# An attention and mixture-of-experts kernel: experts' rows padded to 64 instead of 128, in 64 full slots and 8 mixed ones

## The chip, the cores and the metric

The kernel runs on one core of a Trainium2 chip. The engines are TensorE (PE, with its weight loads shown apart as PEld), VectorE (DVE), ScalarE (ACT), GpSimd (POOL) and SyncE (SP); SP and ACT issue direct transfers on a queue of their own, POOL issues the indexed ones. The metric is the device time of one execution in microseconds (us), median of the runs. In the profile a float32 matmul stands as two records (each goes over its columns twice), so four matmuls are eight records.

## What is computed

A layer on T = 2048 tokens of width 512: layer norm, a gated-delta attention with 8 heads and its residual, a second layer norm, and then a mixture of 16 experts, 4 of them per token, beside a shared expert. The part that matters:

```python
cw = _combine_weights(xt, gate_w)            # [T, 16], four nonzero per token
out = jnp.zeros_like(xt)
for e in range(16):
    a = _swiglu(xt @ expert_up_w[e].T)       # 512 -> 2 x 352 -> 352
    out = out + cw[:, e:e + 1] * (a @ expert_down_w[e].T)   # 352 -> 512
out = out + _swiglu(xt @ shared_up_w.T) @ shared_down_w.T
x = x + out
```

All of it is float32. With the inputs of the reference the 16 experts get 521, 591, 568, 472, 458, 474, 495, 434, 522, 578, 522, 527, 510, 482, 495 and 543 rows, 8192 together; these counts are worked out from the reference and stand in no profile.

## The kernel before

**The order of the work.** The attention runs first (`attention`), with pieces of the shared expert between its matmuls. `experts` then finishes the shared expert (`up`, `down`, `gated`), routes the rows (`routing`: VectorE makes for every row and choice its position in `slot_rows`, and the lists that say which expert a slot has), and GpSimd scatters the rows to `slot_rows` with 64 indexed transfers (L2064). Then come the slots.

**A slot** is 128 rows of one expert. `NQ` = 79 slots are always run: 64 full tiles' worth of rows and 15 for padding, since every expert is padded to a multiple of 128. With the counts above 72 of them hold rows and the last seven are empty; they cost TensorE the same. Every engine walks through `body(q, par)` for all q, by `run_slots` (straight code for the first two and last slots, a loop over pairs between). For one slot:

- TensorE: `gate` (4 matmuls of 352 columns, L2289), `up` (4 of 352, L2298), and then `down` of the slot before (3 of 512, L2314). Gate q waits for `xsT` (s_xT), up q for `a` of the slot before (s_a), down q-1 for its 16 transposed blocks (s_aT).
- ScalarE, in this order: issue the four transfers that load the rows of slot q+2 (`load_rows`, L2106, `xs`, packets of 512 B), issue the small one with weights and indices of slot q+1 (`load_meta`, L2113), SiLU of gate q (L2129), and y of slot q-1 (L2140), scaled out of PSUM.
- VectorE: transpose the rows of slot q+1 (L2175, `xsT`), a = g * up (L2208), transpose a in 16 blocks (L2187), take the combine weights and indices (L2198, L2199).
- GpSimd: one indexed transfer adds the 128 rows of y to `out` (L2079, "rows_added" s_add); each waits for the one before, since two may touch the same row. Rows whose index is out of bounds are left out.
- SyncE: holds three experts' weights in `w` (NS = 3) and loads expert s into w[s % 3] with three transfers (`load_expert`, L32 to L36), once the last slot of expert s-3 is through TensorE (s_yp against the list `tiles_to`). One expert is 512 x 704 and 352 x 512 float32, 2.16 MB.

The list of experts by slot is made by VectorE in `routing` behind the positions (L1896 to L1907).

Of the kernel before, what the change touches and what calls it, by code (L numbers as in the profile page):

```python
# [1781 lines left out]
NQ = K * T // P + E - 1  # L1782
assert NQ % 2 == 1
NS = 3

def routing(nc, es, counts, scratch, lg, xall, pos, qslot, qexp, tiles_to, s_pos, s_read, s_routed, route, s_xall):
# [21 lines left out]
    nti, idle = sb("nti", [P, E], I32), sb("silu_first", [P, E])  # L1808
    nt, one_e, tinc, posf = part(E), part(E), part(E), part(NT, E)
    pj, ids = part(NT, K), part(NT)  # L1810
    idi = sb("idi", [P, NT], I32)
    qi, qc = sb("qi", [1, NQ]), both[0:1, 0:NQ * E].rearrange("p (q e) -> p q e", e=E)
    qf, q3 = sb("qf", [1, NQ]), sb("q3", [1, NQ])
# [10 lines left out]
    def route_pool(pool):  # L1824
        pool.memset(before[:, :], 1.0).then_inc(s_k, 1)
        pool.memset(ones[:, :], 1.0).then_inc(s_k, 1)
        pool.iota(qi[:, :], pattern=[[1, NQ]], base=0, channel_multiplier=0,
# [15 lines left out]

    def route_dve(dve):
        n = [0]

        def mark(ins):
            ins.then_inc(s_d, 1)
            n[0] += 1
# [9 lines left out]
        for step in range(7):  # L1859
# [12 lines left out]
        link(dve.tensor_tensor(cnt[:, :, :], inc[:, :, :], cnt[:, :, :], ALU.subtract))  # L1872

        link(dve.tensor_scalar(nti[:, :], inc[:, :, NT - 1], float(P - 1), None, ALU.add))
        link(dve.tensor_scalar(nti[:, :], nti[:, :], 7, None, ALU.logical_shift_right))
        link(dve.tensor_scalar(nt[:, :], nti[:, :], 1.0, None, ALU.max))
        link(dve.tensor_tensor_scan(tinc[:, :], one_e[:, :], nt[:, :], 0.0, ALU.mult, ALU.add))
        link(dve.tensor_copy(tiles_to[:, :], tinc[0:1, :]))
        link(dve.tensor_tensor(nt[:, :], tinc[:, :], nt[:, :], ALU.subtract))
        link(dve.scalar_tensor_tensor(out=cnt[:, :, :], in0=nt[:, :].unsqueeze(2).to_broadcast([P, E, NT]),  # L1880
                                      scalar=float(P), in1=cnt[:, :, :], op0=ALU.mult, op1=ALU.add))
        dve.tensor_tensor(posf[:, :, :], pre[:, :].rearrange("p (t e) -> p t e", e=E),
                          cnt[:, :, :].rearrange("p e t -> p t e"), ALU.add).then_inc(s_read, 1)
        dve.wait_ge(s_read, 1)
        for j in range(K):
# [10 lines left out]
        dve.wait_ge(s_k, 4)  # L1896
        link(dve.tensor_tensor(qc[:, :, :], qi[:, :].unsqueeze(2).to_broadcast([1, NQ, E]),
                               tinc[0:1, :].unsqueeze(1).to_broadcast([1, NQ, E]), ALU.is_ge))
        link(dve.tensor_reduce(qf[:, :], qc[:, :, :], AX.X, ALU.add))  # L1899
        link(dve.tensor_scalar(qf[:, :], qf[:, :], float(E - 1), None, ALU.min))  # L1900
        link(dve.tensor_copy(qexp[:, :], qf[:, :]))

        link(dve.tensor_copy(q3[:, :], qf[:, :]))
        for m in range(NS, E, NS):
            link(dve.tensor_scalar(qc[:, :, 0], qf[:, :], float(m), -float(NS), ALU.is_ge, ALU.mult))
            link(dve.tensor_tensor(q3[:, :], q3[:, :], qc[:, :, 0], ALU.add))
        dve.tensor_copy(qslot[:, :], q3[:, :]).then_inc(s_routed, 1)  # L1907

    return route_act, route_pool, route_pe, route_dve


def experts(nc, es, wup_d, wdn_d, xs_d, acc_d, x2n_d, xT_d, lg, pos, qslot, qexp, tiles_to, wsh, route, sh, out):
# [11 lines left out]
    w = sb("w", [P, NS, UPW + DNW])  # L1924
    acc = sb("acc_all", [P, NT - EARLY_TILES, D])
# [48 lines left out]
    def first(q):  # L1974
        return isinstance(q, int) and q == 0
# [433 lines left out]
```

## Time and profile before

| | us |
|---|---|
| median of 3 runs (1309.14 to 1313.19) | 1310.31 |
| span of the profiled execution | 1306.4 |
| TensorE busy, share of the span | 1264.5, 97% |
| VectorE, ScalarE, GpSimd busy | 872.4, 375.1, 340.0 |
| from the first slot's gate to the end | 588.0 (718.4 to 1306.4) |

The profiled execution's span is 3.9 us under the median. The profile shows one execution; "busy" of TensorE is modelled from pipelined records. "Granted clock" 1.00 is 2.4 GHz, 0.50 is 1.2 GHz.

### The profile page before, as it was taken

Reading aid. Unit: us, or ns where it says so; the run is one execution under the profiler, and the core shown is the slowest. Engines: PE = TensorE matmul, PEld = TensorE weight load, DVE = VectorE, ACT = ScalarE, POOL = GpSimd, SP = SyncE. Lnnn points to the kernel's source line nnn. Section 1 sums busy time; section 2 is a strip of 40 time slices with the busy share of each in tenths; the row PEclk is TensorE's granted clock in tenths of the full one; section 3 lists DMA queues with packets and bytes.
Section 4 is the critical chain, followed back from the end, with each engine's and each line's share of the span. In section 5 each row is a group of like instructions: output and inputs, shape, how many; then the busy total and the mean of one; then the engine's idle time right before and its main releaser. Section 6 shows DMA issues by size and latency. Waiting matters only on the chain.

```text
span 1306.4 us, 27873 instructions
## 1 busy us (share of the span) xinstructions
PE 1264.5 (97%) x8725; PEld 787.1 (60%) x8726; DVE 872.4 (67%) x2430; ACT 375.1 (29%) x822; POOL 340.0 (26%) x398
## 2 busy tenths in 40 slices
PE   8969999999999999999999999999999999999997
PEld 7857778777775555444444555555555555555553
DVE  4897688768768465262111777777777777777774
ACT  4745655645553333210000111111111111111111
POOL 1301234313242231225651112121212122121212
PEclk9989999999997999999999999999999999999999
DMA  5524944743643694585467456666665656564420
GB/s 163 95 47 99 157 94 101 166 105 85 138 109 114 169 199 116 124 274 199 182 211 246 85 130 138 134 137 137 137 139 133 135 132 136 127 139 72 75 49 9
DMA packets 208516, 171.09 MB, mean 131 GB/s; under 512 B 71472, under 2 KB 160560, under 8 KB 208432
## 3 DMA queue, kind: packets, MB, share of 16 engines
q1 hardware_dynamic: 135056, 114.16, 33.9%
q0 software_dynamic: 16496, 34.23, 13.4%
q10 hardware_dynamic: 56880, 21.54, 7.9%
q8 instruction: 57, 0.93, 0.3%
q14 instruction: 27, 0.22, 0.1%
HBM read 91.06 MB, written 82.73 MB: 133 GB/s over the span
## 4 chain that ended last, share of the span: by engine, by line
PE 55%; DVE 2%; issue 0%; DMA 0%; POOL 0%; ACT 0%; DVEq 0%; POOLq 0%
PE pD L2314 15%; PE pG L2289 14%; PE pU L2298 14%; PE pG L2246 3%; PE pU L2246 3%; PE pD L2265 3%; PE pU L2240 1%; PE pD L2260 0%; DVE ups L2187 0%; DMA out<-y,ix 0%; DVE w L1887 0%; DVE w L1888 0%; DVE route_keep L1886 0%; POOL out L2079 0%; DVE qf L1899 0%
## 5 line engine op out<-in xcount | busy, mean ns | idle before, releaser
L2187 DVE STREAM_TRANSPOSE ups<-a 32x96 f32<-32x96 f32 (+1 forms) x1248 | 326.1, 261 | 42.5
L2079 POOL DMA_INDIRECT out<-y,ix x79 | 123.0, 1557 | 479.1 <-ACT y L2140 319.4
L2314 PE MATMUL pD<-w,ups 128*128 (+1 forms) x474 | 216.6, 592 | 0.7 <-DVE ups L2187 0.7
L2289 PE MATMUL pG<-w,xsT 128*128 x632 | 199.9, 458 | 0.0
L2298 PE MATMUL pU<-w,xsT 128*128 x632 | 199.9, 459 | 0.0
L2289 PEld LDWEIGHTS pG<-w,xsT 128*128 128x128 f32 x632 | 119.5, 189 | 88.4 <-issue 37.4
L2298 PEld LDWEIGHTS pU<-w,xsT 128*128 128x128 f32 x632 | 120.1, 190 | 66.9
L976 PE MATMUL pProj<-front_region 128*128 128x256 f32 x624 | 154.8, 391 | 2.2 <-ACT front_region L711 1.6
L2314 PEld LDWEIGHTS pD<-w,ups 128*128 128x128 f32 (+1 forms) x474 | 90.0, 190 | 93.2 <-issue 76.8
L976 PEld LDWEIGHTS pProj<-front_region 128*128 128x128 f32 x624 | 113.3, 191 | 20.1 <-ACT front_region L711 2.1
L2140 ACT ACTIVATE y<-pD,wq 128x512 f32<-128x512 f32 x79 | 54.3, 687 | 247.0 <-PE pD L2314 234.1
L2129 ACT ACTIVATE g<-pG 128x352 f32<-128x352 f32 x79 | 36.7, 464 | 259.9 <-DVE ix L2199 132.0
L1399 DVE SCALAR_TENSOR_TENSOR front_region<-front_region,cw 128x256 f32<-128x256 f32 x216 | 102.6, 516 | 8.8 <-ACT front_region L747 6.3
L2208 DVE TENSOR_TENSOR a<-g,pU 128x352 f32<-128x352 f32 x79 | 41.2, 521 | 87.2 <-PE pU L2298 79.4
L2064 POOL DMA_INDIRECT slot_rows<-xall,pos x64 | 62.9, 982 | 52.3 <-DMA slot_rows<-xall,pos 47.1
L636 POOL TENSOR_TENSOR TT<-TT,ng 128x512 f32<-128x512 f32 x16 | 17.3, 1082 | 213.7 <-ACT TT L789 137.3
L2175 DVE STREAM_TRANSPOSE xsT<-xs 128x512 f32<-128x512 f32 x79 | 55.9, 708 | 6.2 <-DMA xs<-slot_rows 5.0
L1175 PE MATMUL pT<-wo,oT 128*128 128x512 f32 x128 | 59.1, 604 | 0.4 <-ACT oT L816 0.4
L2265 PE MATMUL pD<-front_region 128*128 128x512 f32 x120 | 53.1, 597 | 0.0
L746 ACT ACTIVATE front_region<-pProj 128x256 f32<-128x256 f32 x78 | 30.1, 386 | 79.0 <-PE pProj L976 76.8
L1461 DVE TENSOR_TENSOR Rs<-pC,vh 64x512 f32<-64x512 f32 x32 | 22.0, 687 | 45.3 <-PE pC L1086 45.0
L2246 PE MATMUL pG<-front_region 128*128 128x512 f32 x112 | 50.4, 593 | 0.6 <-PEq L383 0.6
(258 smaller groups left out, 1661.8 us busy)
## 6 DMA issues: line engine op xcount, KB each, us to landing
w<-in_up_T SPq DMA_DIRECT2D x16, 1408.0 KB
slot_rows<-zeros SPq DMA_DIRECT2D x79, 266.0 KB
xs<-slot_rows ACTq DMA_DIRECT2D x316, 64.0 KB
w<-in_down_T SPq DMA_DIRECT2D x16, 512.0 KB
front_region<-in_L_attn_hidden_states SPq DMA_DIRECT2D x16, 256.0 KB, 3.6
x2r<-in_L_attn_hidden_states SPq DMA_DIRECT2D x16, 256.0 KB, 4.5
partial_sums<-x2r SPq DMA_DIRECT2D x16, 256.0 KB, 2.9
x_normed<-x2n SPq DMA_DIRECT2D x16, 256.0 KB, 2.0
```

Of the source, the lines that this page charges most:

```text
L976: mm = pe.matmul(proj_bank(g), w3[:, w, k, cols(i % DC, P)], xnT[p % 2][:, k, :], start=(k == 0), stop=(k == DC - 1))
L1175: mm = pe.matmul(pT1[:, 0, :], oT[:, k, :], wo[:, k, :], start=(k == 0), stop=(k == DC - 1))
L1399: ins = dve.scalar_tensor_tensor(out=acc[(g + h) % len(acc)], in0=raw[:, at, j:j + PW], scalar=cw[:, at, j:j + 1], in1=acc[(g + h) % len(a ...
L2064: pool.indirect_dma_start(out=xs_d[:, :], out_offset=bass.IndirectOffsetOnAxis(ap=pos[:, i, j:j + 1], axis=0), in_=xall[:, i, :], in_offse ...
L2079: pool.indirect_dma_start(out=flat, out_offset=bass.IndirectOffsetOnAxis(ap=ix[1 - par][:, 0:1], axis=0), in_=y[1 - par][:, :], in_offset= ...
L2175: dve.transpose(xsT[par][:, :, :].rearrange("p k (a i) -> p a k i", a=BLOCKS), xs[par][:, :].rearrange("p (a k j) -> p a k j", a=BLOCKS, k ...
L2187: dve.transpose(aT[par][B * to:B * to + B, 0:n, rows], a[rows, 0:len(IC) * P].rearrange("p (c n) -> p c n", c=len(IC))[:, 0:n, B * to:B * ...
L2246: mm = pe.matmul(p[:, :], wsh["up"][:, k, at:at + P], xg[gr % 2][:, k, :], start=(k == 0), stop=(k == DC - 1))
L2265: mm = pe.matmul(sdown(j)[:, :], sa[:, c, P * i:P * i + P], wsh["down"][:, c, :], start=False, stop=(c == UNITS - 1))
L2289: mm = pe.matmul(pG[0][:, 0:I], xsT[par][:, k, :], w[:, bass.ds(slot, 1), 2 * I * k:2 * I * k + I], start=(k == 0), stop=(k == DC - 1))
L2298: mm = pe.matmul(pU[0][:, 0:I], xsT[par][:, k, :], w[:, bass.ds(slot, 1), 2 * I * k + I:2 * I * (k + 1)], start=(k == 0), stop=(k == DC - 1))
L2314: mm = pe.matmul((pYlast if end(q) else pYq)[:, :], aT[1 - par][0:m, c, :], down[0:m, :, UPW + D * c:UPW + D * (c + 1)], start=(c == 0), s ...
```

## The change

Rows of an expert are now padded to 64. An expert's whole 128-row blocks go to the 64 full slots (NF); what is left, at most 64 rows, goes to a half block, and 16 half blocks make 8 mixed slots (NM), each with two halves of any two experts. If the experts have more than 64 whole blocks together, the ones beyond go to half blocks as well. 72 slots are run instead of 79; every ninth slot, from q = 7, is mixed (7, 16, ..., 70), slot 71 is a full one.

- TensorE, mixed slot (`project`, `bring_down`): each matmul is made as two of 64 stationary columns, for rows 0 to 63 with the one expert's weights, and for rows 64 to 127 with the other's, written to the two halves of the PSUM partitions.
- Weights of mixed slots have a place of their own, `wm`, in the region that held the shared expert's weights. ScalarE issues their loads (`load_mixed`, two experts, six transfers) at the end of its body of slots 0, 9, 18, ..., 63, after y. The full slots' loads stay with SyncE, but their expert is now read from a list (`source`), and so is the slot after which they may start (`until`).
- GpSimd adds a mixed slot with two indexed transfers, one for each half, one after the other.
- `routing` has about 9 more small operations and 6 on 256 columns ahead of the positions; the lists are made in five pieces (`list_dve`) between VectorE's operations of the shared expert. s_routed now comes from the fifth, and all three first weight loads wait for it.
- The slots are written out straight instead of in a loop, and TensorE reads two register values for the slot before where it read one.

The core of the diff:

```diff
+HR = P // 2
+NF = K * T // P
+NM = E // 2
+NQ = NF + NM
+STEP = NQ // NM
+MIXED = STEP - 2
+def is_mixed(q):
+    return q % STEP == MIXED
+    wm = region[:, 0:2 * (UPW + DNW)].rearrange("p (h n) -> p h n", h=2)
@@ run_slots
-        with eng.Fori(1, (NQ - 3) // 2) as pair:
-            body(2 * pair, 0)
-            body(2 * pair + 1, 1)
+        for q in range(NQ + 1):
+            body(q, q % 2)
@@ sync
-                load_expert(sp, w[:, s % NS], wup_d[s], wdn_d[s], s_w)
+                load_expert(sp, w[:, s % NS], *weights_from(sp, "source", s), s_w)
@@ gpsimd
+                for h in range(2 if is_mixed(q - 1) else 1):
+                    to = ixm[h] if is_mixed(q - 1) else ix[1 - par]
+                    least(pool, s_add, 16 * (adds_before(q - 1) + h))
+                    pool.indirect_dma_start(...)
@@ scalar
+            def load_mixed(m):
+                for h in range(2):
+                    load_expert(act, wm[:, h], *weights_from(act, "mixed", 2 * m + h), s_wm)
@@ scalar, end of body(q, par)
+                if q % STEP == 0 and q < NQ:
+                    if first(q):
+                        act.wait_ge(s_routed, 1)
+                    load_mixed(q // STEP)
@@ tensor
+            def project(out, rows, q, weights, at):
+                if is_mixed(q):
+                    for k in range(DC):
+                        for h in range(2):
+                            half = slice(HR * h, HR * h + HR)
+                            mm = pe.matmul(out[half, 0:I], rows[:, k, half], wm[:, h, 2 * I * k + at:2 * I * k + at + I],
+                                           start=(k == 0), stop=(k == DC - 1))
+                    return mm
+            def bring_down(out, gated_, q, weights, c):
+                m, at = IC[c], UPW + D * c
+                if is_mixed(q):
+                    for h in range(2):
+                        half = slice(HR * h, HR * h + HR)
+                        mm = pe.matmul(out[half, :], gated_[0:m, c, half], wm[0:m, h, at:at + D],
+                                       start=(c == 0), stop=(c == 2))
+                    return mm
```

ScalarE's instructions from one y to the next, in the loop of before (`xs` the rows, `mt` weights and indices, `g` the SiLU; ISA rows are register work):

```order
L2140 ACTIVATE y<-pD,wq 128x512 [waits rows_added]
L2106 ISA [waits slotsT_ready]
L2106 DMA xs<-slot_rows 32x4x128
...
L2113 ISA [waits meta_taken]
L2113 DMA mt<-slot_rows 128x20
L2129 ACTIVATE g<-pG 128x352 [waits gated_ready,gate_psum]
```

And the same stretch of the changed kernel after slot 8's y, in the body of slot 9 (`front_region` holds `wm`):

```order
L2248 ACTIVATE y<-pD,wq 128x512 [waits rows_added,meta_taken,y_psum2]
L2092 TENSOR_LOAD list_mixed
L32 DMA front_region<-in_up_T 128x4x704
L34 DMA front_region<-in_down_T 128x2x512
L36 DMA front_region<-in_down_T 96x512
...
L2211 DMA xs<-slot_rows 32x4x128 [waits slotsT_ready]
L2211 DMA xs<-slot_rows 32x4x128 x3
L2217 DMA mt<-slot_rows 128x20 [waits meta_taken]
L2238 ACTIVATE g<-pG 128x352 [waits gated_ready,gate_psum]
```

Between y of slot 8 and the loads of slot 12's rows now stand the six transfers of two experts' weights, on the same queue.

TensorE's instructions at a mixed slot of the changed kernel, from its gate to the gate of the next (`pG`, `pU`, `pD` are the PSUM banks of gate, up and down):

```order
L2405 MATMUL pG<-front_region,xsT 64x352 [waits gate_silu,mixed_weights_loaded,slotsT_ready]
L2405 MATMUL pG<-front_region,xsT 64x352 x7
...
L2405 MATMUL pU<-front_region,xsT 64x352 [waits gated_ready]
L2405 MATMUL pU<-front_region,xsT 64x352 x7
L2422 ISA [waits y_ready,gatedT_ready]
L2422 MATMUL pD<-w,ups 128x512
...
L2409 MATMUL pG<-w,xsT 128x352
```

Eight half matmuls stand for four whole ones in gate and up, then the down of the full slot before; the mixed slot's own down (six half matmuls) follows after the next up.

## Rows read from the trace of the kernel before

**Rows 1.** The costliest groups: count, busy us, mean ns, and idle before.

```profile
L2314 PE MATMUL pD<-w,ups 128*128 (+1 forms) x474 | 216.6, 592 | 0.7 <-DVE ups L2187 0.7
```

**Rows 2.** Timeline of one slot: start, us, engine, line, what; idle before in brackets.

```profile
782.66 2.53 PE L2289 MATMUL pG<-w,xsT 128*128 x8
782.95 0.69 ACT L2140 ACTIVATE y<-pD,wq 128x512 f32<-128x512 f32 x1 [3.26 <-PE pD L2314]
...
788.31 4.64 DVE L2187 STREAM_TRANSPOSE ups<-a 32x96 f32<-32x96 f32 x16
...
789.98 2.53 PE L2289 MATMUL pG<-w,xsT 128*128 x8
...
793.15 0.71 DVE L2175 STREAM_TRANSPOSE xsT<-xs 128x512 f32<-128x512 f32 x1
...
794.71 2.74 PE L2314 MATMUL pD<-w,ups 128*128 x6
...
797.29 2.53 PE L2289 MATMUL pG<-w,xsT 128*128 x8
...
797.53 0.37 SPq L32 DMA_DIRECT2D w<-in_up_T  x1
```

**Rows 3.** Timeline, TensorE, four 64 x 64 tiles in turn.

```profile
35.68 0.69 PE L1037 MATMUL pG<-kq 64*64 64x64 f32 x32
36.30 0.48 PE L976 MATMUL pProj<-front_region 128*128 128x256 f32 x1
```

**Rows 4.** Timeline, TensorE: two row halves of 512 columns, then whole matmuls.

```profile
582.34 1.13 PE L2260 MATMUL pD<-front_region 64*128 64x512 f32 x4
583.40 1.12 PE L2265 MATMUL pD<-front_region 128*128 128x512 f32 x2
```

**Rows 5.** One line's weight loads, 64 columns: duration ns min/median/max.

```profile
L1189 PEld LDWEIGHTS pT<-gw,x2g x256: 132/138/227, 194.8 to 553.0; 128*64 128x64 f32 x128
```

**Rows 6.** Transfers issued from 555.9 to 562.9 us, median us from issue to landing.

```profile
front_region<-x2n_turned SPq DMA_DIRECT2D x4, 256.0 KB, 9.4
```

**Rows 7.** Transfers issued from 584 to 592 us.

```profile
front_region<-x2n_turned SPq DMA_DIRECT2D x4, 256.0 KB, 3.8
```

**Rows 8.** GB/s in 40 slices of 550 to 570 us.

```profile
GB/s 0 0 0 0 0 0 0 0 0 33 119 127 111 397 397 389 414 373 377 303 393 418 397 324 389 414 393 389 354 339 323 299 292 291 295 320 359 393 381 389
```

**Rows 9.** Transfers during an expert's weight load, 797 to 805 us, 40 slices.

```profile
GB/s 0 0 0 0 0 0 0 84 113 84 70 99 282 324 296 261 284 370 413 399 397 419 342 385 352 411 410 404 348 310 344 312 298 327 335 353 315 318 279 333
...
out<-y,ix POOLq DMA_INDIRECT x1, 8.1
```

**Rows 10.** The page: adds, median us to landing.

```profile
out<-y,ix POOLq DMA_INDIRECT x79, 4.8
```

**Rows 11.** Adds issued from 1285 to 1306 us.

```profile
out<-y,ix POOLq DMA_INDIRECT x3, 2.7
```

**Rows 12.** Timeline, the last two adds.

```profile
1296.56 1.56 POOL L2079 DMA_INDIRECT out<-y,ix  x1 [6.09 <-ACT y L2140]
...
1300.19 1.55 POOL L2079 DMA_INDIRECT out<-y,ix  x1 [2.07 <-DMA out<-y,ix]
```

**Rows 13.** TensorE by stretches: length, busy (records), granted clock, transfers' share, GB/s.

```profile
87.50:90.50 3.00, 0.03 (x1) 0.99 0.00 0
90.50:93.20 2.70, 0.02 (x1) 0.50 0.00 0
93.20:97.30 4.10, 4.10 (x41) 0.50 0.01 4
...
298.70:302.10 3.40, 3.40 (x26) 0.50 0.67 141
```

**Rows 14.** Register reads of the slot list: duration ns min/median/max.

```profile
L2270 PEldq TENSOR_LOAD <-qslot x79: 296/305/987, 706.9 to 1283.2; - x79
```

**Rows 15.** Timeline, VectorE: a routing operation on 256 columns, slot 0's rows.

```profile
577.30 0.42 DVE L1872 TENSOR_TENSOR w<-w 128x256 f32<-128x256 f32 x1
...
711.27 0.71 DVE L2175 STREAM_TRANSPOSE xsT<-xs 128x512 f32<-128x512 f32 x1 [1.77 <-DMA xs<-slot_rows]
```

More of the change, by code:

```diff
@@ L1781, with before_mixed, adds_before, block_of @@
 NE = E + 2
-NQ = K * T // P + E - 1
-assert NQ % 2 == 1
-NS = 3
-def routing(nc, es, counts, scratch, lg, xall, pos, qslot, qexp, tiles_to, s_pos, s_read, s_routed, route, s_xall):
+HR = P // 2
[4 more added lines that the diff above has]
+MIXED = STEP - 2
+NS = 3
+def is_mixed(q):
+    return q % STEP == MIXED
+def before_mixed(q):
+    return max(0, (q + STEP - 1 - MIXED) // STEP)
+def adds_before(q):
+    return q + before_mixed(q)
+def block_of(q):
+    return NF + q // STEP if is_mixed(q) else q - before_mixed(q)
+assert sorted(block_of(q) for q in range(NQ)) == list(range(NQ))
+assert all(q == i + (i + 1) // 8 for q in range(NQ) if not is_mixed(q) for i in [block_of(q)])
+def routing(nc, es, counts, scratch, lg, xall, pos, lists, s_pos, s_read, s_routed, route, s_xall):
     def sb(name, shape, dt=F32):
@@ L1807, in routing @@
     cnt, seg, inc = part(E, NT), part(E, NT), part(E, NT)
-    nti, idle = sb("nti", [P, E], I32), sb("silu_first", [P, E])
-    nt, one_e, tinc, posf = part(E), part(E), part(E), part(NT, E)
+    hti, fti, idle = sb("hti", [P, E], I32), sb("fti", [P, E], I32), sb("silu_first", [P, E])
+    hf, ff, of, cumf, cumo, one_e = (part(E) for _ in range(6))
+    full_rows, odd_at, apart, over, posf = part(E), part(E), part(E), part(1), part(NT, E)
     pj, ids = part(NT, K), part(NT)
     idi = sb("idi", [P, NT], I32)
-    qi, qc = sb("qi", [1, NQ]), both[0:1, 0:NQ * E].rearrange("p (q e) -> p q e", e=E)
-    qf, q3 = sb("qf", [1, NQ]), sb("q3", [1, NQ])
+    qi, qc = sb("qi", [1, NF]), both[0:1, 0:NF * E].rearrange("p (q e) -> p q e", e=E)
+    qf, qa, q3 = sb("qf", [1, NF]), sb("qa", [1, NF]), sb("q3", [1, NF])
+    cap, had, some, nth, twice, le, lm, lo_ = (sb(n, [1, E]) for n in (
+        "cap", "had", "some", "nth", "twice", "list_e", "list_m", "list_o"))
+    done_i = sb("done_i", [1, E], I32)
     pre, tot = counts[:, 0:NT * E], counts[:, NT * E:2 * NT * E]
@@ L1914, in experts @@
+    return route_act, route_pool, route_pe, route_dve, list_dve
+def experts(nc, es, wup_d, wdn_d, xs_d, acc_d, x2n_d, xT_d, lg, pos, lists, region, wsh, route, sh, out):
     N = GN
@@ L2121, in body @@
                     load_rows(1, 1)
-                if not (isinstance(q, int) and q >= NQ - 2):
+                if q < NQ - 2:
                     load_rows(q + 2, par)
@@ L2334, in program @@
         pos = es.enter_context(nc.sbuf_tensor("pos", [P, NT, K], I32))
-        qslot = es.enter_context(nc.sbuf_tensor("qslot", [1, NQ], I32))
-        qexp = es.enter_context(nc.sbuf_tensor("qexp", [1, NQ], I32))
-        tiles_to = es.enter_context(nc.sbuf_tensor("tiles_to", [1, E], I32))
+        lists = {name: es.enter_context(nc.sbuf_tensor(f"list_{name}", [1, n], I32)) for name, n in (
+            ("slot", NF), ("load", NF), ("expert", NF), ("source", E), ("until", E), ("mixed", E))}
         xs_d = nc.dram_tensor("slot_rows", (NQ * P, RW), F32, kind="Internal").ap()
```

267 lines of the change are left out of this document (168 added, 99 removed).

## The prediction

> **What bounds the kernel now.** I read the costliest groups first, then the timeline of one slot. TensorE does: its largest group waited 0.7 us in 474 records [rows 1], and in the slots one gate begins 7.31 us after the other (782.66, 789.98, 797.29) with gate, up and down end to end [rows 2]. The other engines fit into that time. For what the change adds on the queues I need more: how long after ScalarE's y of a slot q-1 (T0, 782.95) the next steps are due [rows 2]. The gate beside it, at 782.66, is that of slot q+1, so the gate at 797.29 is that of slot q+3: due at T0+14.34. VectorE transposes its rows at T0+10.2. VectorE's 16 transposes take 4.64 and end at T0+10.0, the down that needs them starts at T0+11.76: 1.8 us of slack.
>
> **The change, part by part.**
>
> *Seven slots less.* 79 become 72, at 7.31 each: -51.2 us, all on TensorE's path.
>
> *Half matmuls.* A mixed slot has twice the matmuls, of 64 stationary columns each. It costs nothing more if the two halves run at the same time. Nothing before has column halves with long operands; the nearest are 16 matmuls on four tiles of 64 x 64 (two row halves times two column halves) [rows 3]: 32 records, each of 64 columns gone over twice (128 cycles at 2.4 GHz, 0.053), would be 1.7 us one after the other and 0.85 if only the row halves ran together; they take 0.62. So column halves do run together, and I take 7.31 for a mixed slot. To it comes the change of tiling: two row halves of 512 columns hold TensorE from 582.34 to 583.40, 1.06, where two rounds of 1024 cycles need 0.85 [rows 4]: 0.2 per change. A mixed slot changes four times (into gate and up, out, into its down, out): 0.8 x 8 = +6.4, bounds 0 and 6.4.
>
> *Adds.* A mixed slot has two, in turn. In the middle the second lands about 11 us after the slot's y (two steps of 3.6 to 4.8 and a landing [rows 10, 12]), and what waits for it lies within VectorE's 1.8 us of slack: 0, at most 1 us per slot. At the end it counts: slot 70 is mixed, and slot 71's add stands behind both. One add more is 3.63 us [rows 12]; and the last add had no rows before (2.7 us to landing [rows 11]) and has rows now (4.8 [rows 10]), 2.1. Sum +5.7.
>
> *Routing.* Six operations on 256 columns at about 0.45 [rows 15] and some nine small ones make the scatter 4 us later, and with it slot 0's rows. They were there at 711.27 [rows 15], the gate at 718.4: covered, 0; without that cover it would be +4. The lists lie between operations of an idle VectorE, and the register reads (0.3 us, at most 0.99 [rows 14]) are done by TensorE's sequencer while matmuls run: 0.
>
> *The mixed weights' loads.* This is the term that decides. ScalarE issues 2 x 2.16 = 4.33 MB right after y of slot q-1, q = 0, 9, ..., 63, and behind it, on the same queue, the rows of slot q+3. What does a small transfer behind large ones cost? Four of 256 KB took 9.4 us to landing behind 3 MB of SyncE's own, against 3.8 with nothing large ahead [rows 6, 7]. So a queue is served in order, and the rows wait for the last byte of both experts. The rate of large transfers alone is about 389 GB/s [rows 8].
> Without another load: first byte at T0+2.3 (a register read, the issue, and 1.0 us as SyncE's load shows, issued at 797.53 and seen from 798.5 [rows 2, 9]); 4.33 MB and one add's 0.26 MB take 11.8, T0+14.1; the rows' 512 small packets and their landing 1.4; the transpose 0.8 [rows 2]: T0+16.3 against 14.34, 2.0 late. VectorE then makes a (0.5) and its transposes (4.64), 0.5 more than gate and up cover: 2.5 us.
> With an expert's load of SyncE beside it: from the reference's counts the full blocks give loads after slots 4, 10, 14, 19, 23, 28, 32, 36, 40, 46, 50, 55 and 59 are done, the mixed ones start after 9, 18, 27, 36, 45, 54 and 63. So six of the seven (not 63) meet one: five times it comes 7.3 us later, once at the same time. First byte T0+9.3; by then 2.46 MB of the mixed weights are in, 1.87 remain, and shared in equal parts this takes 2 x 1.87 + 0.26 (an add) = 4.0 MB, 10.3 us, T0+19.6. Rows T0+21.0, transposed T0+21.8: 7.5 late, and 0.5 for the transposes, 8.0. The sixth comes to the same within 1 us.
> The load of slot 0 starts at 722 with gate 3 due at 738.8, late enough: 0. Sum 6 x 8.0 + 2.5 = +50.5. Bounds: 0, if the rows were not held up, and 6 x 10 + 5 = 65, if adds and issue stretch it.
>
> *The clock.* TensorE stands still some 7 us in each of the six. Before, a still stretch of 5.7 us ended with a granted clock of 0.50, and 4.1 us of work then ran at it; another fall lasted 3.4 us, busy throughout [rows 13]. Half speed for 4.1 us costs 2.05, of which 0.5 hides the wait for the transposes: 6 x 1.55 = +9.3, bounds 0 and 15.
>
> *Sum.* 1306.4 - 51.2 + 6.4 + 5.7 + 50.5 + 9.3 = 1327.1 of span; the median stood 3.9 over the span: 1331.
>
> **A rule weighed.** TensorE's weight loads of 64 columns took 0.138 [rows 5], and in rows 3 they hide behind the matmuls, since 4 tiles with loads and matmuls keep 0.62 for 32 records. The Trainium skill, "TensorE: Matmul & The Clock Gate", Part 3 on packing small matmuls, says that a weight load overlaps with matmuls in flight only where the row group differs; two column halves share all rows. The trace disagrees (0.62 us in rows 3). By the rule the sum would be rival C's first time, by the trace it stays.
>
> **Rivals.**
> *A, faster: the rows are not held up much.* Place: gate q+3 in the bodies of slots 9 to 63. If the six transfers leave gaps that the rows use, or SyncE's load gets less than an equal part, each of seven stalls is 2.5 at most and the clock stays up: 1306.4 - 51.2 + 6.4 + 5.7 + 17.5 + 3.9 = 1289, and 1271 with none. For it: under SyncE's load ScalarE's rows still came, since they are on another queue. Against: rows 6. It decides from an average of 6.5 us per met load, clock included: above, the kernel is slower than before.
> *B, the stalls are half as long (4.5 us),* since an add or the rows need less: 27 + 2.5, half the clock's price: 1306.4 - 51.2 + 6.4 + 5.7 + 29.5 + 5 + 3.9 = 1306.
> *C, it doesn't do what it says: column halves don't overlap in full.* Weight loads exposed: a mixed slot has 22 rounds, 22 x 0.138 x 8 = 24 more, 1355. Halves one after the other: 8 x 7.3 = 58 more, 1389. Against both: rows 3; for them: no operand there is longer than 64 columns.
>
> **How the numbers follow.** Forecast 0.54 (1316 to 1346), A 0.24 (1270 to 1297), B 0.13 (1298 to 1315), C 0.09 (1347 to 1395). A measurement of this kernel tells about 0.3% from no change: faster is under 1306.4, slower over 1314.2. Faster: A and 0.07 of B, 0.31; same 0.06; slower 0.63. The range leaves out the lower third of A and most of C: 1283 to 1358.
>
> **What would show it.** Right: after slots 9, 18, ..., 54 TensorE stands for 6 to 9 us at the gate three slots on, with VectorE's `xsT` waiting for the transfer of `xs`, and ScalarE's queue moving 4.3 MB just before; granted clock 0.50 there; about 2 us after slot 63, nothing after slot 0. A mixed slot's gate as long as a full one's (2.35 us from start to start). Last add about 5 us later behind the last y than before. Wrong: stalls under 4 us with the rows landing within 16 us of y (A, B); 64-column records that start alone, one after the other, or a mixed slot of more than 9 us (C); or slot 0's rows later than its gate.

## The result, and the profile of the changed kernel

| | before | changed |
|---|---|---|
| median of four runs, us | 1310.66 (1309.14 to 1313.19) | 1364.18 (1358.73 to 1366.32) |
| span of the profiled execution | 1306.4 | 1357.0 |

The ratio is 1.0405, 95% interval 1.0379 to 1.0431: slower by 4%. The prediction said 1331 and a range of 1283 to 1358. The direction was right, the size was not. The profiled execution of the changed kernel is the fastest of its four (1358.73), 5.5 us under their median, so the spans differ by 50.6 and the medians by 53.5. The page of the changed kernel (busy us and share; then the chain that ended last, by engine and by line):

```profile
span 1357.0 us, 25907 instructions
...
PE 1245.9 (92%) x8747; PEld 757.5 (56%) x8747; DVE 845.2 (62%) x2352; ACT 366.0 (27%) x808; POOL 340.4 (25%) x401
...
PE 43%; DMA 8%; ACTq 5%; issue 1%; DVE 0%; ACT 0%; POOLq 0%
PE pD L2422 9%; PE pG L2409 9%; PE pU L2409 8%; DMA xs<-slot_rows 8%; PE pD L2390 4%; PE pG L2371 4%; PE pU L2371 4%; ACTq L2211 2%; PE pD L2419 2%; PE pG L2405 1%; PE pU L2405 1%; ACTq L34 1%; ACTq L36 1%; ACTq L32 1%; PE pU L2365 1%
```

TensorE's busy time fell by 18.6 us, far less than the 51.2 of seven slots, because part of what is left ran at half speed (the same instructions are busy for 1221.1 us in the kernel of the first experiment, where TensorE hardly waits, and for 1245.9 here); and the chain now holds the rows' transfer and ScalarE's own issuing (ACTq). The waits of TensorE in the slots (engine, line, releaser: us in all, times, longest):

```profile
PE pG L2409 <- ACT g L2238: 45.8, 7, 11.3
PE pG L2409 <- DVE xsT L2287: 18.7, 7, 4.8
```

Seven mixed loads, each with a stall at gate q+2, and behind six of them a second one at gate q+3 (the seventh wait for `xsT`, 0.41 us at slot 3, is not behind one of these loads; the load after slot 62's y has only the first stall, 3.14). This is the first, after slot 8's y (timeline: start, us, engine, line; idle before in brackets), to be read beside [rows 2]:

```profile
794.55 2.53 PE L2409 MATMUL pG<-w,xsT 128*128 x8
794.75 0.69 ACT L2248 ACTIVATE y<-pD,wq 128x512 f32<-128x512 f32 x1 [3.79 <-PE pD L2422]
795.43 0.42 ACTq L32 DMA_DIRECT2D front_region<-in_up_T  x1
...
798.35 1.50 ACTq L34 DMA_DIRECT2D front_region<-in_down_T  x1
...
800.00 0.54 ACTq L36 DMA_DIRECT2D front_region<-in_down_T  x1
800.58 9.64 ACTq L2211 DMA_DIRECT2D xs<-slot_rows  x4
802.83 0.37 SPq L32 DMA_DIRECT2D w<-in_up_T  x1
...
810.26 1.46 ACTq L2217 DMA_DIRECT2D mt<-slot_rows  x1
811.83 0.46 ACT L2238 ACTIVATE g<-pG 128x352 f32<-128x352 f32 x1 [16.39 <-issue]
...
812.54 4.09 PE L2409 MATMUL pG<-w,xsT 128*128 x8 [10.52 <-ACT g L2238]
...
821.89 0.71 DVE L2287 STREAM_TRANSPOSE xsT<-xs 128x512 f32<-128x512 f32 x1 [4.12 <-DMA xs<-slot_rows]
...
823.05 2.63 PE L2409 MATMUL pG<-w,xsT 128*128 x8 [1.47 <-DVE xsT L2287]
```

The gate at 794.55 is slot q+1's (q = 9). Its SiLU, which stands in ScalarE's program behind all eleven issues, came at 811.83 and not at about 797. Of the 16.39 us before it, 9.64 went into issuing four transfers of 64 KB; without a large load ahead, the same four took 1.76. So **the engine that issues is held, not only the data**: gate q+2 waited 10.52 for g. Then the rows came late as well, and gate q+3 waited 1.47. This load is one of the two with the longest hold. From the first weight issue to the SiLU it is 9.0 to 16.9 us in the seven, and the hold does not always stand in the rows' issues, which took 2.8 to 5.6 behind the other six: at 1034.35 the six weight issues themselves took 10.2. The gate at 812.54 took 4.09 instead of 2.53: the clock had fallen.

```profile
core 0: us, PE busy (x), PEclk, DMA share, GB/s
801.50:811.70 10.20, 0.52 (x2) 0.69 1.04 351
812.60:815.00 2.40, 2.40 (x4) 0.50 1.05 324
```

Two terms of the prediction stand nearly as they were sized. A mixed slot, gate to gate 7.57 (772.01, 779.58) and 7.55 (779.58, 787.13), each some 0.25 over 7.31; the interval before these is 0.09 longer and the one behind them 0.11, 0.70 in all:

```profile
772.01 2.59 PE L2405 MATMUL pG<-front_region,xsT 128*64 128x352 f32 x16
774.43 2.54 PE L2405 MATMUL pU<-front_region,xsT 128*64 128x352 f32 x16
776.89 2.84 PE L2422 MATMUL pD<-w,ups 128*128 x6
779.58 2.53 PE L2409 MATMUL pG<-w,xsT 128*128 x8
...
784.40 2.80 PE L2419 MATMUL pD<-front_region,ups 128*64 128x512 f32 x12
787.13 2.63 PE L2409 MATMUL pG<-w,xsT 128*128 x8
```

Sixteen half records take 2.42 from start to start, where eight whole ones take 2.36: the halves overlap in full. And the end, three adds in turn, the last 5.74 us behind the start of the last y (before, the last add at 1300.19, [rows 12], stood 2.6 behind its y):

```profile
1341.47 1.56 POOL L2185 DMA_INDIRECT out<-y,ix_mixed  x1 [6.55 <-ACT y L2248]
1342.77 0.69 ACT L2248 ACTIVATE y<-pD,wq 128x512 f32<-128x512 f32 x1 [2.08 <-PE pD L2422]
1344.93 1.55 POOL L2185 DMA_INDIRECT out<-y,ix_mixed  x1 [1.91 <-DMA out<-y,ix_mixed]
1348.51 1.56 POOL L2185 DMA_INDIRECT out<-y,ix  x1 [2.02 <-DMA out<-y,ix_mixed]
```

### The profile page after: what moved, and what is told of

It reads as the page before. It is cut to its first block, busy times and chain, and to the rows that moved or that the text cites. A ratio compares the mean times of both kernels' runs of the same rounds, so it can differ in the third digit from the quotient of the medians.

```text
span 1357.0 us, 25907 instructions
## 1 busy us (share of the span) xinstructions
PE 1245.9 (92%) x8747; PEld 757.5 (56%) x8747; DVE 845.2 (62%) x2352; ACT 366.0 (27%) x808; POOL 340.4 (25%) x401
## 3 DMA queue, kind: packets, MB, share of 16 engines
q0 software_dynamic: 16640, 34.24, 12.2%
## 4 chain that ended last, share of the span: by engine, by line
PE 43%; DMA 8%; ACTq 5%; issue 1%; DVE 0%; ACT 0%; POOLq 0%
PE pD L2422 9%; PE pG L2409 9%; PE pU L2409 8%; DMA xs<-slot_rows 8%; PE pD L2390 4%; PE pG L2371 4%; PE pU L2371 4%; ACTq L2211 2%; PE pD L2419 2%; PE pG L2405 1%; PE pU L2405 1%; ACTq L34 1%; ACTq L36 1%; ACTq L32 1%; PE pU L2365 1%
## 5 line engine op out<-in xcount | busy, mean ns | idle before, releaser
L2298 DVE STREAM_TRANSPOSE ups<-a 32x96 f32<-32x96 f32 (+1 forms) x1136 | 296.9, 261 | 35.4
L2409 PE MATMUL pG<-w,xsT 128*128 x512 | 181.5, 501 | 64.6 <-ACT g L2238 45.8
L2185 POOL DMA_INDIRECT out<-y,ix x64 | 99.6, 1557 | 451.4 <-ACT y L2248 308.1
L2409 PEld LDWEIGHTS pG<-w,xsT 128*128 128x128 f32 x512 | 103.7, 206 | 149.9 <-issue 113.9
L2422 PE MATMUL pD<-w,ups 128*128 (+1 forms) x384 | 176.9, 596 | 0.7 <-DVE ups L2298 0.7
L2409 PE MATMUL pU<-w,xsT 128*128 x512 | 163.3, 462 | 0.0
L2409 PEld LDWEIGHTS pU<-w,xsT 128*128 128x128 f32 x512 | 98.6, 193 | 56.3 <-issue 3.8
L2422 PEld LDWEIGHTS pD<-w,ups 128*128 128x128 f32 (+1 forms) x384 | 71.8, 190 | 80.2 <-issue 70.2
L2248 ACT ACTIVATE y<-pD,wq 128x512 f32<-128x512 f32 x72 | 49.4, 687 | 198.3 <-PE pD L2422 174.4
L2287 DVE STREAM_TRANSPOSE xsT<-xs 128x512 f32<-128x512 f32 x72 | 50.8, 705 | 47.6 <-DMA xs<-slot_rows 47.4
```

Of the source, the lines that this page charges most:

```text
L2185: pool.indirect_dma_start(out=flat, out_offset=bass.IndirectOffsetOnAxis(ap=to[:, 0:1], axis=0), in_=y[1 - par][:, :], in_offset=None, bou ...
L2248: act.activation(y[1 - par][:, :], (pYlast if end(q) else pYq)[:, :], ACT.Copy, scale=wq[1 - par][:, 0:1]).then_inc(s_y, 1)
L2287: dve.transpose(xsT[par][:, :, :].rearrange("p k (a i) -> p a k i", a=BLOCKS), xs[par][:, :].rearrange("p (a k j) -> p a k j", a=BLOCKS, k ...
L2298: dve.transpose(aT[par][B * to:B * to + B, 0:n, rows], a[rows, 0:len(IC) * P].rearrange("p (c n) -> p c n", c=len(IC))[:, 0:n, B * to:B * ...
L2409: mm = pe.matmul(out[:, 0:I], rows[:, k, :], w[:, bass.ds(weights[0], 1), 2 * I * k + at:2 * I * k + at + I], start=(k == 0), stop=(k == D ...
L2422: return pe.matmul(out[:, :], gated_[0:m, c, :], w[0:m, bass.ds(weights[0], 1), at:at + D], start=(c == 0), stop=(c == 2))
```

## Experiments

Each stands beside runs of the kernel before on the same chip (medians 1310.65 to 1311.24); ratios are to those. The edits shift lines by a few, so gate is L2409 in one kernel and L2411 or L2414 in another; names tell. A cut diff shows the core of an edit; where the same change touches several lines, only one kind of them stands here. Two theories at the start: **Q**, ScalarE's queue (a long queue holds the engine that issues, and the rows lie behind 4.3 MB); **B**, the bytes themselves, which share 16 DMA engines whoever issues them.

**The loads alone.** Only the first pair is loaded.

```diff
-                if q % STEP == 0 and q < NQ:
-                    if first(q):
-                        act.wait_ge(s_routed, 1)
-                    load_mixed(q // STEP)
+                if first(q):
+                    act.wait_ge(s_routed, 1)
+                    load_mixed(0)
```

> The changed kernel, but only the first mixed slot's two experts are loaded; the seven later mixed slots use them again (their rows are computed with the wrong experts, all else is as before). Both theories expect the time without what the seven loads cost: 1310.3 - 51.2 for seven slots + 5.6 for the changes of tiling + 5.4 for the adds at the end, 1270, within 1266 to 1276, with TensorE never waiting between slot 1 and slot 70. If the column halves or the straight code cost more than the trace of the changed kernel seems to show, it stays above 1285.

Measured 1270.25 (1269.23 to 1272.37), ratio 0.9693 (0.9668 to 0.9717); TensorE has one gap over 0.5 us in all slots (0.73, at slot 0). Seven later loads cost the whole 94 us between this and 1364. The rest of the change is worth 40.

**Another placement of the same bytes.** One expert three slots after the other:

```diff
-                if q % STEP == 0 and q < NQ:
+                if q % STEP in (0, 3) and q < NQ:
-                    load_mixed(q // STEP)
+                    load_mixed(q // STEP, q % STEP // 3)
```

> The changed kernel, with the second expert of a mixed slot loaded by ScalarE three slots after the first: same bytes, same queue, never more than 2.16 MB ahead of the rows. Theory Q (ScalarE's queue: its packets fill it, the issue of the next rows then holds ScalarE's instruction stream, and the rows lie behind 4.3 MB): 864 + 512 + 128 packets no longer fill the queue, no SiLU is late, and the rows lie behind 5.6 us of weights, with another 5.6 where SyncE loads an expert as well: 0 to 10 us of stalls in all, 1270 to 1282. Theory B (bytes: 34 MB more share 16 engines, whatever the queue and the place): as the changed kernel, 1350 to 1370.

On SyncE's queue:

```diff
+            def load_mixed(m):
+                least(sp, s_g, 1)
+                least(sp, s_yp, STEP * m)
+                for h in range(2):
+                    load_expert(sp, wm[:, h], *weights_from(sp, "mixed", 2 * m + h), s_wm)
+            ahead_of = {3: (0,), 4: (1,), 6: (2,), 8: (3,), 10: (4,), 12: (5,), 14: (6,)}
             for s in range(NS, E):
+                for m in ahead_of.get(s, ()):
+                    load_mixed(m)
...
+            load_mixed(NM - 1)
```

> The changed kernel, with the mixed slots' weights issued by SyncE, at the same slots and in one go as before, between the experts' loads. Theory Q: ScalarE's queue holds only rows and indices again, which share the engines with one stream of weights instead of lying behind it: no issue above 2 us on ScalarE, waits of TensorE under 15 us in all, 1270 to 1290 (adds are slower for longer, that is the upper end). Theory B: 1350 to 1370.

And in six pieces of 0.72 MB, still by ScalarE (`load_piece` issues two of the four chunks of up, or down, of one expert):

```diff
-                if q % STEP == 0 and q < NQ:
+                if q % STEP < 6 and q < NQ:
-                    load_mixed(q // STEP)
+                    load_piece(q // STEP, q % STEP)
```

> The changed kernel, with the two experts of a mixed slot loaded by ScalarE in six pieces of 0.72 MB, one each at the end of six slots in a row. Theory Q: a row's transfer lies behind 1.9 us of weights at most, inside the slack of 4 us: no wait of TensorE, 1268 to 1276. Theory B: the same bytes cost the same, 1350 to 1370.

Measured 1298.78 (1296.55 to 1304.83), 1296.96 (1295.37 to 1304.18) and 1301.56 (1301.28 to 1303.29); ratios 0.9899 (0.9873 to 0.9925), 0.9898 (0.9867 to 0.9930), 0.9930 (0.9906 to 0.9955). Both theories missed, from two sides. B is refuted as the main cause: the same seven pairs, 30.3 MB, cost 27 to 31 us over 1270 instead of 94. Q is right for two thirds, and something remains, of nearly the same size in three placements. It isn't the same thing in all three. With the loads on SyncE's queue TensorE waits at gates, 15.4 us in the slots:

```profile
PE pG L2411 <- ACT g L2244: 6.9, 7, 2.3
PE pG L2411 <- DMA w<-in_up_T: 4.4, 2, 2.4
PE pG L2411 <- DMA w<-in_down_T: 4.1, 2, 2.2
```

The waits put down to the weights are the SiLU's as well: each of these four gates starts 0.25 us after the end of a late SiLU (g from 957.84 for 0.46, the gate at 958.55), and that SiLU stood behind VectorE's index taking. With one expert at a time on ScalarE's queue, 12.2 of 21.7 us follow a late transposition of rows (`xsT`), so the rows still came late behind the queue. With six pieces no gate of a full slot waits for g at all: 13.6 us are at the mixed slots' own gates, all seven, and 11.6 at six gates that wait for `xsT`.

**What the halves cost.** In the one-load kernel, gate and up with the halves one after the other, and then with whole matmuls.

```diff
-                    for k in range(DC):
-                        for h in range(2):
+                    for h in range(2):
+                        for k in range(DC):
```

> The one-load kernel (only the first mixed pair is loaded, later mixed slots reuse it, so their rows meet the wrong experts), with gate and up of a mixed slot written as four matmuls of the one half and then four of the other, instead of in turn. Down stays in turn. If two halves overlap only where their matmuls stand next to each other: a full gate is 2.35 and a full up 2.35 from start to start, so the two become 4.7 longer per mixed slot, 38 us in eight, 1270 + 38 = 1308. If the hardware could run them together in any order, or if weight loads alone set the price: 1270 as before, down to 1267 with fewer alternations.

Measured 1282.10 (1280.69 to 1283.85), ratio 0.9776 (0.9754 to 0.9798): 12 more, neither 0 nor 38. TensorE's timeline of that kernel shows why (gate at 771.56, the next operation's first matmul at 774.04, while matmuls of the gate still start at 774.92):

```profile
771.56 2.93 PE L2404 MATMUL pG<-front_region,xsT 128*64 128x352 f32 x13
774.04 0.51 PE L2404 MATMUL pU<-front_region,xsT 128*64 128x352 f32 x1
774.33 0.46 PE L2404 MATMUL pG<-front_region,xsT 128*64 128x352 f32 x1
...
774.92 0.46 PE L2404 MATMUL pG<-front_region,xsT 128*64 128x352 f32 x1
774.98 2.88 PE L2404 MATMUL pU<-front_region,xsT 128*64 128x352 f32 x13
```

TensorE starts the second half while the last records of the first half still run, and up while gate does. The order in the code costs 1.34 per mixed slot from gate to gate (8.91 against 7.57), 1.5 by the medians, not 4.7.

```diff
-                    for k in range(DC):
-                        for h in range(2): ...
+                    for k in range(DC):
+                        mm = pe.matmul(out[:, 0:I], rows[:, k, :], wm[:, 0, ...], ...)
```

> The one-load kernel with whole matmuls (128 stationary columns, the first half's weights) in the mixed slots: leaves out that the second half has its own expert. It takes the whole price of halves away and nothing else. From the slots of the one-load kernel (y to y 0.70 more around a mixed slot) both theories expect 8 x 0.70 = 5.6 less: 1264.6. If nothing moves, the 0.70 was the two adds' or the table's; if 10 or more come off, halves cost something beyond their slots, such as the clock.

Measured 1268.22 (1264.84 to 1270.66), ratio 0.9663 (0.9638 to 0.9687). The mixed slot is back at 7.31 from gate to gate (774.70 to 782.01 to 789.32 in its trace); the median moved by 2, its interval touches that of the one-load kernel, and this profile has three small stalls more (0.74, 1.30 and 0.81 us) and its first gate 4.1 us later (721.97 against 717.86). The 0.70 per slot is confirmed in the trace, not by the medians.

**The remainder on SyncE's queue: who waits for what.** In the SyncE kernel VectorE waits 57.0 us, 26 times, for an add of y to land before it may take indices. So, without the adds of slots 0 to 68, and with deeper buffers:

```diff
-                if first(q):
+                if q - 1 < 69:
                     return
```

(and `adds_before`, which the waits go by, counts from slot 69 on).

> SyncE issues the mixed loads, as in the run before of that name (1297), and the indexed adds of slots 0 to 68 are left out, so that out lacks their rows; the last adds stay. Adds theory (what is left of the loads' price is that the weights' bytes slow the adds, whose ends VectorE's index taking waits for): 1270 to 1275, and no wait for them. Bytes theory (the rows of xs come late because the engines' share is short): 1288 to 1297, with xsT still waiting for xs; the adds' own bytes, 0.26 MB each, give back 1 or 2 at most.

```diff
-    y = [sb(f"y{i}", [P, D]) for i in range(2)]
+    y = [sb(f"y{i}", [P, D]) for i in range(2)] + [region[:, FRONT_W - D:FRONT_W]]
-                    least(act, s_add, 16 * adds_before(q - 2))
+                    least(act, s_add, 16 * adds_before(q - 3))
-                least(dve, s_add, 16 * adds_before(q - 1))
+                least(dve, s_add, 16 * adds_before(q - 2))
```

> SyncE issues the mixed loads, and y, wq and ix are three deep, so that taking indices and y of a slot wait for the adds two and three slots back instead of one and two. Nothing is left out. Adds theory: most of the 27 us between 1297 and 1270 comes back: 1270 to 1280, since the queue of adds catches up between loads. Bytes theory: 1290 to 1297.

Without adds: 1268.03 (1266.95 to 1271.69), ratio 0.9679 (0.9654 to 0.9703), all of the remainder gone, and no gate waits. Three deep: 1293.25 (1290.90 to 1293.59), ratio 0.9863 (0.9844 to 0.9882): 4 back, not 20, and the interval of the ratio overlaps that of two deep. I took the depth to be still too small, and made it four; beside it the same for the two kernels with ScalarE's loads.

> SyncE issues the mixed loads and y, wq and ix are four deep. Nothing is left out. With three deep the worst stall came where a mixed slot's two adds in turn, each of about 8 us under the weights' bytes, ended 6.9 us after VectorE wanted the indices' place. One slot more of room is 7.3 us. Adds theory: that stall and nearly all others go, 1270 to 1276 (1268 to 1272 as without adds or loads, plus a few steps of 0.5). Bytes theory (xs or the weights themselves late): 1285 to 1293, as three deep.

Measured 1297.03 (1292.99 to 1307.69), ratio 0.9880 (0.9854 to 0.9905). Wrong again: no gain. The trace is of the slowest of the five executions (1307.69), so its sizes are on the long side. The timeline shows what the depth can't mend (a mixed slot's two adds, VectorE's index taking, SiLU, gate):

```profile
941.11 1.57 POOL L2196 DMA_INDIRECT out<-y,ix_mixed  x1 [8.42 <-DMA out<-y,ix]
...
949.85 1.55 POOL L2196 DMA_INDIRECT out<-y,ix_mixed  x1 [7.17 <-DMA out<-y,ix_mixed]
...
957.56 0.15 DVE L2323 COPY wq<-mt 128x1 f32 x1 [9.27 <-DMA out<-y,ix_mixed]
...
958.19 1.56 POOL L2196 DMA_INDIRECT out<-front_region,ix  x1 [6.79 <-DVE ix L2324]
...
958.25 0.46 ACT L2244 ACTIVATE g<-pG 128x352 f32<-128x352 f32 x1 [11.96 <-DVE ix L2324]
...
958.96 2.71 PE L2411 MATMUL pG<-w,xsT 128*128 x4 [6.09 <-ACT g L2244]
```

From one add's issue to the next it is 8.74 and 8.34 us here, while TensorE makes a slot in 7.31. Over this trace, 80 adds are issued between 738.50 and 1297.41, a mean step of 7.07; 27 of the 79 steps are over 8 us (mean 9.5, while weights come in) and 43 are between 5.3 and 6.3. The chain of adds is a **second bound**: each waits for the one before, and it hardly pauses. Only nine of the 79 steps ended with GpSimd released by y; they took 54.8 us together, 3.8 more than steps of 5.7 would have. The three-deep kernel, whose trace is of its fastest execution, has the same picture: 79 steps in 545.6 us, mean 6.91, ten of them released by y, 6.3 us over steps of 5.7. TensorE's 72 slots need 532 (72 x 7.31 + 8 x 0.70).

> ScalarE issues the mixed loads in six pieces of 0.72 MB, one after each of six slots, as in the run before of that name (1302), now with y, wq and ix four deep. Adds theory: as there, most of the 30 us over 1270 comes back, 1270 to 1280. If ScalarE's share of issuing (its rows 2.2 us behind a piece) is what is left there: 1290 to 1302, with VectorE's xsT waiting for xs.

Measured 1301.72 (1298.48 to 1309.39), ratio 0.9917 (0.9895 to 0.9939), as with two deep (1301.56). Depth doesn't help here either, but not for the reason above: it is the second half of the expectation that came true. The chain of adds has room here (29 of its 79 steps were released by y, 44.7 us over steps of 5.7), and TensorE's waits in the slots are for something else:

```profile
PE pG L2414 <- issue: 16.4, 7, 3.8
PE pG L2418 <- DVE xsT L2296: 10.2, 6, 3.0
```

L2414 is a mixed slot's gate, and "issue" says that the profile shows no releaser; the time fits the landing of its own weights. At slot 16 the last piece was issued at 837.00 and landings took up to 7.4 us there; the gate, due at 842.5, started at 844.49. So the last piece very likely came too late for the slot that needs it. Pieces that start a slot earlier were not tried.

**Number, bytes or meeting?** Four deep, with one add per mixed slot (its second half's rows left out):

```diff
-                for h in range(2 if is_mixed(q - 1) else 1):
+                for h in range(1):
```

(and `adds_before(q)` is q).

> As the four-deep run with SyncE's mixed loads at the old place, but a mixed slot is added with one indexed transfer instead of two; the rows of its second half are left out. All weights are still loaded, 8 of 80 adds are gone. Chain theory: 72 adds at a mean of 6.9 need 497 us, less than TensorE's 533: 1270 to 1278. If it is the adds' bytes or what they do to the weights: the bytes fall by 5% alone, 1290 or more.

Measured 1264.58 (1263.28 to 1265.82), ratio 0.9644 (0.9627 to 0.9661). All weights are loaded, 72 adds instead of 80, and every gap but slot 0's 0.72 is gone. GpSimd now waits for y more often, which means that the chain has room. The rows below are for the two of four y buffers that go by that name, and 30.3 of the 84.4 us is the wait before the first add; over both names and without that one, y released 16 of 71 steps, with 91 us of idle GpSimd, against 9 of 79 steps with 41 us four deep with 80 adds.

```profile
POOL out L2196 <- DMA out<-y,ix: 145.6, 24, 9.3
...
POOL out L2196 <- ACT y L2254: 84.4, 10, 30.3
```

Of the 32 us under the four-deep kernel, one step, 3.6, is that the last add stands behind one less.

The pair's loads three slots later, away from the two adds of the mixed slot, four deep and two deep:

```diff
-                least(sp, s_yp, STEP * m)
+                least(sp, s_yp, STEP * m + 3 if m else 0)
-            ahead_of = {3: (0,), 4: (1,), 6: (2,), 8: (3,), 10: (4,), 12: (5,), 14: (6,)}
+            ahead_of = {3: (0,), 5: (1,), 7: (2,), 9: (3,), 11: (4,), 13: (5,), 15: (6,)}
```

> SyncE issues the mixed loads, y, wq and ix four deep, and the pair for mixed slot 9m+7 starts after slot 9m+2 instead of 9m-1, so not while the two adds of mixed slot 9m-2 run. Nothing is left out. In the four-deep run before (1297) a step from one add to the next took 8.3 to 11 us under weights and 5.6 to 6 between, and the 80 steps filled the slots' time, so that depth bought nothing. Chain theory (the adds, each waiting for the one before, are now the bound): bytes and number of adds are the same, so the mean step hardly falls; but the queue of adds is emptied before each load: 1275 to 1290. Burst theory (only the meeting of load and double add hurts): 1270 to 1276.

> SyncE issues the mixed loads after slot 9m+2, all buffers as in the changed kernel (two deep). Chain theory: the queue of adds can run only one slot late before VectorE waits for it, so more is lost than four deep: 1282 to 1300. Burst theory: 1270 to 1280. It tells whether the place or the depth does the work.

Measured 1291.55 (1289.02 to 1292.08), ratio 0.9847 (0.9828 to 0.9865), and 1292.71 (1292.33 to 1294.20), ratio 0.9865 (0.9848 to 0.9881). Against the old place (1297.03 and 1296.96) that gives some 4 to 5 us, and the intervals of the ratios overlap at each depth: the meeting of load and double add is a small part at most, and depth is worth nothing that can be told. The burst theory is out. Nothing is left out in either, and they are faster than both kernels: 1.3 to 1.5% under before.

**Back to the changed kernel.** With four deep, and without adds (edits as above), ScalarE's burst in place:

> The changed kernel as it is (ScalarE issues the six transfers at once) with y, wq and ix four deep: takes the adds out of its stalls and leaves ScalarE's queue. Queue theory for the changed kernel: its stalls start from ScalarE held in issuing and from rows behind 4.3 MB, not from adds, so little comes back: 1345 to 1364. If the adds were also what held the changed kernel: 1335 or less, as of the 94 us for loads 27 remained with the queue free.

> The changed kernel with ScalarE's burst, and the adds of slots 0 to 68 left out. Queue theory for the changed kernel: both stalls stay, 64 us of still TensorE and 20 of slow clock; the adds' 0.5 MB within each burst are gone: 1345 to 1362. If adds were a large part there too, as with the loads on SyncE (28 us): 1335 or less.

Measured 1364.24 (1358.26 to 1365.08), ratio 1.0391 (1.0358 to 1.0423), and 1349.89 (1347.21 to 1351.06), ratio 1.0290 (1.0271 to 1.0309). Without the adds 14 of the 94 us come back and 80 stay; TensorE's gaps go from 65 to 54. The adds also lengthen the hold: without them it is 7.9 to 12.1 us from the first weight issue to the SiLU. Then the hold itself, by the number of pieces:

```diff
-                  up.rearrange("(c p) n -> p c n", p=P)
+                  up.rearrange("(p c) n -> p (c n)", p=P)
```

(and the same for down's first 256 rows).

> The changed kernel, but each partition reads one run of consecutive rows of in_up_T (11 KB) and of in_down_T (4 KB), so the same bytes in 128 + 128 + 96 pieces per expert instead of 512 + 256 + 96; the mixed rows then meet weights in the wrong order. Pieces theory (ScalarE is held since its queue takes only so many pieces at once): the hold of 9.6 us in issuing xs shrinks to 2 or less, the stall at gate q+2 (64.5 us in all for it and 18.7 for the second) goes, the rows still lie behind the bytes: the second stall grows to about 8, 1330 to 1350 in all. Bytes theory: the hold is as long as before, 1358 to 1370; if long pieces are cut into short ones on the way, the same.

Measured 1366.49 (1361.93 to 1368.54), ratio 1.0407 (1.0380 to 1.0435): not faster at all, where I had forecast 1330 to 1350. But the two stalls trade places, as the pieces theory says. TensorE's waits and ScalarE's timeline in this kernel:

```profile
PE pG L2414 <- DVE xsT L2292: 65.5, 8, 11.2
PE pG L2414 <- ACT g L2243: 9.3, 7, 2.6
```

```profile
801.43 2.20 ACTq L2211 DMA_DIRECT2D xs<-slot_rows  x4
803.67 1.56 ACTq L2217 DMA_DIRECT2D mt<-slot_rows  x1
805.34 0.46 ACT L2243 ACTIVATE g<-pG 128x352 f32<-128x352 f32 x1 [8.45 <-issue]
...
807.03 10.07 ACTq L2211 DMA_DIRECT2D xs<-slot_rows  x3
...
824.04 0.71 DVE L2292 STREAM_TRANSPOSE xsT<-xs 128x512 f32<-128x512 f32 x1 [12.41 <-DMA xs<-slot_rows]
...
825.11 3.30 PE L2414 MATMUL pG<-w,xsT 128*128 x5 [11.09 <-DVE xsT L2292]
```

The first four xs issues take 2.20 instead of 9.64, so SiLU comes at 805.34, and in all seven loads 6.3 to 8.5 us behind the first weight issue instead of 9.0 to 16.9; the hold comes one body later (10.07 for three here, the longest of the seven); and the rows of slot q+3 land no sooner, since the same bytes are ahead of them. With the same bytes ahead, the transposition of slot q+3's rows ended 28.6 us after y here and 27.9 in the changed kernel. So in these two kernels the number of pieces decides when ScalarE is held, and the bytes ahead in the queue when the rows come; the late rows alone cost what both stalls cost together (74.8 us of waits here, 64.5 there).

## Why the prediction was off

| term, us | forecast | in the trace |
|---|---|---|
| seven slots less | -51.2 | -51.2 (slots of 7.31 in both) |
| mixed slots | +6.4 | +5.6 (8 x 0.70) |
| adds at the end | +5.7 | +5.4 |
| routing, front | 0 | +3.1 (not the change's, see below) |
| stalls | +50.5 | +64.5 |
| clock | +9.3 | +23.2 (what remains of the sum; TensorE's busy time is 24.8 over that of the one-load kernel) |
| span against 1306.4 | +20.7 | +50.6 |

- **Slots, halves, end: right.** Whole matmuls bring back 7.31. Rival C is refuted; rivals A and B, with smaller stalls, are out as well, though A's sum without any stall, 1271, is what the one-load kernel runs in (1270.25). The rule of the Trainium skill weighed in the prediction ("TensorE: Matmul & The Clock Gate", Part 3) doesn't hold here: by it, and with rival C's first price, a mixed slot would have cost some 3 us more, and it cost 0.70. Nor does this case agree with the same Part's statement that matmuls start strictly in order: with the halves in sequence, a matmul of up (774.04) starts before the last ones of gate (774.33 to 774.92).
- **Routing: 0 forecast, and 0 is right.** The first gate came 3.1 us later (721.50 against 718.44), but the one-load kernel, with the same routing, has it at 717.86, and the whole-matmul kernel at 721.97. Executions differ by that much before the slots: line 1175, in the attention, first runs at 150.6 before, 155.2 in the changed kernel and 151.4 and 155.8 in these two. Slot 0's rows were transposed at 716.35, 5.1 us ahead of the gate, so the cover held.
- **Stalls: the step that failed is that a load causes a single stall, of 8.0, at gate q+3.** Mechanism, place and trigger of that stall were right (rows in order behind 4.3 MB, SyncE's load beside it at T0+8), but it was taken for the only effect. I priced ScalarE's issues as if they cost their usual time, and did not ask what stands behind them in its own program: the SiLU of slot q+1, on which gate q+2 waits. Gate q+2 waited up to 11.3 us for it. What was forecast as six stalls of 8.0 and one of 2.5 came as 45.8 at gate q+2 behind seven loads and 18.3 at gate q+3 behind six, 9.2 per load. The rows' own delay was too small in the sum as well: transposed 27.9 us after y (821.89 + 0.71 less 794.75), where it had 21.8. That the total, 64.5, is still within the term's upper bound of 65 is luck: most of it is a stall that the prediction did not have. The long-packet kernel shows the forecast mechanism almost alone: six gaps of 7.5 to 11.2, mean 9.9, for the 8.0, and 4.7 for the 2.5 of the last load.
- **Clock: 1.55 per stall was mis-sized.** It took one short interval from before [rows 13], and the term's upper bound was 15. Most loads have two still stretches, and the granted clock was at 0.50 nine times, for 3.4 to 13.7 us, 61 us of the slots in all; some of that lies within the stretches and costs nothing. The loss is 23 by the sum.
- **Adds in the middle, "0, at most 1 us per slot": wrong.** Without them the changed kernel is 14 us faster. I had a landing of 8.1 under a load [rows 9] and used 3.6 to 4.8 for the step.

After all this the answer to where the expected gain went is: 1270 was there for the taking. Of the 94 us that eat it, about 67 go when the loads leave ScalarE's queue (1364 to 1297), and 65 when they stay on it with one expert at a time (1299), so it is the burst there that costs them. The 27 that are left on SyncE's queue go with the adds: a chain that the extra weights slow and the eight extra adds fill (1297 to 1264.6 with eight adds less, 1268 with none). The shares depend on the order: taken out first, with the burst in place, the adds give back 14. What is left in the two other placements was not traced to its end: rows late behind the queue have a part in both, the chain is not full with six pieces, and no run there leaves the adds out. What is left open: whether a chain of 80 adds could be made faster without leaving out rows. It needs a reason why two neighbours may overlap, and none was tried.

## What to carry to other kernels

Before a load is moved to an engine's queue, list what stands behind the issue in that engine's own program, not only what stands behind it in the queue: if the queue is long, compute waits too. And for a chain of transfers that each wait for the last, compare steps times mean step with the time of the loop, the mean taken under the new load, and look whether the chain paused while it was taken: 79 steps in 546 to 559 us, with hardly a pause, against 532 of TensorE is a bound, and three or four buffers in place of two didn't move it.

## What the runs showed of the hardware that I had not expected

- An issue on ScalarE's queue usually takes 0.4 us; behind six weight transfers four small ones took 9.64 together in the worst of seven cases, 2.8 to 5.6 in the others, and the engine did nothing else. It isn't ScalarE's queue alone: SyncE, with these loads on its queue, was held up to 4.11 us in one issue, and behind it stand only weights that are due slots later. With the same bytes in about 350 instead of 864 pieces per expert, those four took 2.20 and a later three 10.07.
- In a chain of indexed adds it is 5.8 us from issue to issue between the weight loads, and 9.5 in the steps over 8 us, which meet weights (the four-deep kernel; 9.3 in the mean with one expert at a time on ScalarE's queue). The Trainium skill, "DMA: Bandwidth & Descriptors", on queues, rings and completion order, says that each DMA engine takes turns between the queues that have work, a packet at a time. The trace agrees in direction (the add's landing is slower though its queue is its own); it doesn't show the turns.
- Column halves of 64 overlap in full with operands of 352 and 512 columns, at 0.70 us per mixed slot, which I put down to its four changes of tiling (the whole-matmul run shows the price, not its reason), and partly even when their matmuls don't stand next to each other.
